# An attention block and a Fourier block on one core: down-projection in steps of 4, 1 and 1 tiles, tables, key buffer, head 0 operands and weights moved, products on unused PSUM banks around the transforms

## The chip, the cores and the metric

The kernel runs on one core of one Trainium2 chip. A core has four compute engines with instruction streams of their own (TensorE, VectorE, ScalarE, GpSimd) and SyncE (SP), which here issues nearly all transfers on one queue served by 16 DMA engines. The metric is device microseconds of one execution; less is better. In names of rows PE is TensorE, DVE VectorE, ACT ScalarE and POOL GpSimd.

## The reference

The input is 1x48x48x192, 2304 tokens of 192 channels. The first layer is a transformer block with 12 heads of 16 channels and a decomposed relative position term; the second is a Fourier block with block-diagonal complex weights. Both end in an MLP of width 768.

```python
xn = layernorm(x, ln1_g, ln1_b)
q, k, v = split(xn @ qkv_w + qkv_b)                    # 12 heads of 16
attn = einsum('bqc,bkc->bqk', q * scale, k)
attn += rel_h[:, :, :, :, None] + rel_w[:, :, :, None, :]  # q times tables Rh, Rw
x = x + (softmax(attn) @ v) @ proj_w + proj_b
x = x + gelu(layernorm(x) @ mlp_w1 + mlp_b1) @ mlp_w2 + mlp_b2
# second layer
h = layernorm(x, g1, be1)
xf = rfft2(h)                                          # 48 x 25 modes
o = softshrink(cmul(relu(cmul(xf, w1) + b1), w2) + b2, 0.01)
h = irfft2(o) + h + x
y = h + gelu(layernorm(h) @ fc1_w + fc1_b) @ fc2_w + fc2_b
```

## The kernel before

The kernel is written by hand, an instruction stream for each engine, with counted semaphores between them. Each engine works in order. Nearly every product is made in float16 pairs: a value is a rounded part (`hi`) and a rest (`lo = x - hi`), and hi and lo have products of their own.

*Stage 1, queries, keys, values.* The tokens come in NC = 6 chunks of 384. VectorE normalises (`norm_chunk`; the inverse root is GpSimd's `norm_root`), TensorE transposes, ScalarE applies gain and bias, TensorE makes keys, queries and values, ScalarE rounds keys and queries into `khl`, VectorE subtracts, and SP stores both parts to DRAM as `kq_d`; `columns_first` on GpSimd makes a copy of the queries in column order (`qw_d`). SP reads the queries back, three heads' worth on 96 partitions (`q_h`, `q_w`). In the first chunks ScalarE and VectorE also prepare the relative tables `rel` (`table_hi`, `table_parts`, `table`); their 12 loads and the 3 of `mask` are issued by ScalarE. In SBUF, `khl` and `rel` lie where the staging tiles `stage` of stage 2 lie.

*Stage 2, relative terms.* For s = 0 to 3 (6 heads by rows, 6 by columns, and again), 8 tiles each, TensorE multiplies queries with tables, ScalarE rounds to `stage_hi`, VectorE subtracts to `stage_lo`, and SP stores both to `rel_d` (2.65 MB for each s). s = 2 needs the tiles of s = 0 stored, s = 3 those of s = 1.

*Stage 3, the heads.* First the maximum of each row of scores is found: units of products of `qc` and `kc` (queries with relative terms, keys with one-hot rows), reduced by VectorE into `mx_p`; the maxima pass through DRAM (`m_d`, function `m_through_dram`) into a row of `qv`. Then, in three quarters of 18 steps for each head, scores from `ka` and `qv`, an exponential on ScalarE, and products with `v_ext`. Between the steps run the maximum units of the next quarter. SP loads the operands of the next quarter or head at counts of `s_ps`, a step each. The MLP weights are loaded before head 0's second quarter, and GpSimd scales and splits them.

*Stage 4, first MLP and width transform* (`block0`), 6 chunks: `up` makes 6 hidden tiles, ScalarE does gelu and `hi`, and the engine that runs `lo_of_hidden` the rest; `down` multiplies. In between stand the projection and normalisation of the next chunk. `down` before starts so:

```python
pe.wait_ge(sems["hi"], (c + 1) * HM - 1)   # 5 of 6 tiles
for t in (0, 2): hi_products(t, range(HM - 1))
pe.wait_ge(sems["hi"], (c + 1) * HM)
```

*Stage 5, transforms along the height and the complex products*, 5 groups of 5 modes, with a way through DRAM before (`u1_d`) and after (`u2_d`). *Stage 6, second MLP* (`block1`), like stage 4, where GpSimd subtracts 4 of the 6 hidden tiles (POOL_TILES) and VectorE 2.

## Time and profile before

| | us |
|---|---|
| median of 3 runs (1145.84 to 1151.11) | 1150.13 |
| the profiled execution | 1151.58 |
| its span | 1149.8 |
| TensorE busy | 1013.9 (88%) |
| VectorE busy | 844.1 (73%) |
| ScalarE busy | 700.7 (61%) |
| GpSimd busy | 181.0 (16%) |
| mean granted clock of TensorE | 0.937 |

The span goes from the first instruction to the last; 1.8 us of the execution lie around it. A clock of 1.00 is 2.4 GHz, 0.50 is 1.2 GHz. Stage 1 lasts to about 74 us, stage 2 to 122, the maxima before head 0 run from 130 and its scores from 159, the heads end at 833, the first MLP at 955, the transforms at 1054. A busy share is a mean over stages with different limits, so each stage has to be read alone.

### The profile page before, as it was taken

The numbers are of one execution on the slowest core, as the hardware profiler recorded it, in microseconds if no ns is written. First come the engines' busy times: TensorE is split into PE (matmuls) and PEld (weight loads), VectorE is DVE, ScalarE is ACT, GpSimd is POOL, SyncE is SP. The second block draws the span as 40 slices with busy tenths as digits, with TensorE's granted clock in tenths as the row PEclk, the third lists the DMA queues.
The fourth block names the chain that finished last, engine by engine and source line by source line (L and its number), as shares of the span: only waits on it lengthen the run. The fifth ranks groups of instructions, "written<-read, shape, count | busy, mean of one in ns | idle before, by whom it ended". The sixth has DMA issues, their size and how long they took to land.

```text
span 1149.8 us, 35628 instructions
## 1 busy us (share of the span) xinstructions
PE 1013.9 (88%) x15434; PEld 725.3 (63%) x15434; DVE 844.1 (73%) x1702; ACT 700.7 (61%) x1002; POOL 181.0 (16%) x154
## 2 busy tenths in 40 slices
PE   4867588999999999999999999999987884984997
PEld 2545135667777776777777776777476763862776
DVE  2846677999999998999999999999246562232442
ACT  3646126777777777778777777777853450322554
POOL 2540008200000000000000000000046461001443
PEclk9985569999999999999999999999999997995999
DMA  8498697656475656566574756646000012111110
GB/s 120 120 248 263 205 174 125 116 91 116 89 120 95 108 93 105 101 96 112 86 122 87 126 85 113 98 79 108 26 11 22 22 32 56 39 45 45 38 38 21
DMA packets 83234, 109.14 MB, mean 95 GB/s; under 512 B 14334, under 2 KB 75459, under 8 KB 82886
## 3 DMA queue, kind: packets, MB, share of 16 engines
q1 hardware_dynamic: 82550, 105.10, 47.3%
q10 hardware_dynamic: 528, 1.77, 1.2%
q8 instruction: 121, 1.98, 0.8%
q14 instruction: 35, 0.29, 0.1%
HBM read 85.40 MB, written 21.44 MB: 93 GB/s over the span
## 4 chain that ended last, share of the span: by engine, by line
PE 74%; DVE 8%; DMA 7%; ACT 4%; issue 2%; POOL 2%; SPq 1%; ACTq 1%; DVEq 0%
PE ps L1003 36%; PE ps L998 18%; PE ps L1157 17%; DVE mx_p L1446 3%; DVE xh L101 2%; ACT hid_f L930 2%; POOL hid L746 1%; PE ps L1011 1%; DVE stage_lo L1418 1%; DMA mask<-in_c_mask 1%; ACT hid L924 1%; DMA m_d<-mneg 1%; DMA rel_d<-stage_lo 1%; PE ps L1103 1%; POOL rstd L109 1%
## 5 line engine op out<-in xcount | busy, mean ns | idle before, releaser
L1446 DVE TENSOR_REDUCE mx_p<-ps 128x1 f32<-128x464 f32 (+1 forms) x1080 | 608.5, 629 | 43.4 <-PE ps L1003 32.5
L880 ACT ACTIVATE prob<-ps 128x768 f32<-128x768 f32 x648 | 496.0, 810 | 194.5 <-PE ps L1003 193.6
L1003 PE MATMUL ps<-kc,qc 112*32 112x464 f16 (+1 forms) x4320 | 463.0, 370 | 15.2 <-DMA qc<-rel_d 11.2
L1003 PE MATMUL ps<-qv,ka 113*32 113x384 f16 x5184 | 405.6, 328 | 13.4 <-DMA qv<-m_d 5.9
L1157 PE MATMUL ps<-prob,v_ext 128*32 128x384 f32 x2592 | 294.5, 487 | 2.0 <-issue 1.5
L1003 PEld LDWEIGHTS ps<-qv,ka 113*32 113x32 f16 x5184 | 217.6, 97 | 88.7 <-issue 30.3
L1003 PEld LDWEIGHTS ps<-kc,qc 112*32 112x32 f16 x4320 | 176.5, 95 | 112.8 <-issue 31.6
L1157 PEld LDWEIGHTS ps<-prob,v_ext 128*32 128x32 f32 x2592 | 118.4, 111 | 16.4 <-issue 3.5
L998 PE MATMUL ps<-w_dn,hid 128*96 128x192 f16 x864 | 78.2, 251 | 13.9 <-ACT hid L924 13.1
L998 PEld LDWEIGHTS ps<-w_dn,hid 128*96 128x96 f16 x864 | 74.5, 126 | 18.7 <-ACT hid L924 16.2
L719 POOL COPY v_ext<-v_all 128x288 f32<-128x288 f32 x12 | 5.1, 428 | 512.8 <-PE ps L1157 512.7
L998 PE MATMUL ps<-xnt_all,w_up 96*128 96x384 f16 x432 | 76.9, 331 | 3.0 <-ACT xnt_all L872 2.2
L746 POOL TENSOR_TENSOR hid<-hid_f,hid 128x384 f16<-128x384 f32 x60 | 59.7, 1003 | 73.1 <-ACT hid L924 72.0
L930 ACT ACTIVATE hid_f<-ps,b_up 128x384 f32<-128x384 f32 x72 | 40.6, 580 | 42.3 <-PE ps L998 42.2
L998 PEld LDWEIGHTS ps<-xnt_all,w_up 96*128 96x128 f16 x432 | 42.2, 99 | 33.9 <-issue 5.8
L109 POOL TENSOR_TENSOR rstd<-rstd 96x4 f32<-96x4 f32 x24 | 24.3, 1013 | 218.4 <-DVE rstd L96 218.0
L868 ACT ACTIVATE xnt_f<-ps,shift,gain 96x384 f32<-96x384 f32 x24 | 14.7, 662 | 64.1 <-PE ps L1011 64.1
L1011 PE MATMUL ps<-ident,xh 96*96 96x96 f32 x144 | 17.9, 276 | 33.3 <-DVE xh L101 24.8
L1424 DVE TENSOR_TENSOR xnt_all<-xnt_f,xnt_all 96x768 f16<-96x768 f32 x12 | 11.5, 955 | 45.1 <-ACT xnt_all L872 45.1
L1418 DVE TENSOR_TENSOR stage_lo<-ps,stage_hi 96x864 f16<-96x864 f32 x32 | 31.2, 1045 | 16.6 <-ACT stage_hi L856 16.6
L856 ACT ACTIVATE stage_hi<-ps 96x864 f16<-96x864 f32 x32 | 27.1, 894 | 21.2 <-DMA kq_d<-khl 8.2
L1011 PEld LDWEIGHTS ps<-ident,xh 96*96 96x96 f32 x144 | 14.4, 142 | 37.0 <-DVE xh L101 19.2
(103 smaller groups left out, 821.1 us busy)
## 6 DMA issues: line engine op xcount, KB each, us to landing
qv<-rel_d SPq DMA_DIRECT2D x216, 144.0 KB
qv<-kq_d SPq DMA_DIRECT2D x108, 216.0 KB
qc<-rel_d SPq DMA_DIRECT2D x24, 216.0 KB, 4.1
xin<-in_x SPq DMA_DIRECT2D x12, 288.0 KB, 3.8
kq_d<-khl SPq DMA_DIRECT2D x24, 144.0 KB, 2.3
q_h<-kq_d SPq DMA_DIRECT2D x9, 288.0 KB, 4.7
q_w<-qw_d SPq DMA_DIRECT2D x9, 288.0 KB, 6.9
rel_d<-stage_hi SPq DMA_DIRECT2D x4, 648.0 KB, 8.4
```

The source lines that it names most:

```text
L101: ins = nc.vector.tensor_scalar(dst[:, t, :], src[:, t, :], mv[:, t, 0:1], rstd[:, 1, t:t + 1], ALU.subtract, ALU.mult)
L109: nc.gpsimd.tensor_tensor(rstd[:, 1, :], rstd[:, 0, :], rstd[:, 2, :], ALU.pow).then_inc(sem["rstd"], 1)
L746: nc.gpsimd.tensor_tensor(hid[:, m, 1, :], hid_f[:, m, :], hid[:, m, 0, :], ALU.subtract).then_inc(sems["lo"], 1)
L856: nc.scalar.activation(out_hi[0], x, ACT.Copy).then_inc(op_hi, 1)
L880: nc.scalar.activation(prob[:, s4(p, s), :].rearrange("p (a b) -> p a b", a=2), ps[:, 3 + 2 * (s % 2):5 + 2 * (s % 2), 0:CW], ACT.Exp).the ...
L930: nc.scalar.activation(hid_f[:, m, :], ps[:, m % 2, 0:CW], ACT.Gelu, bias=b_up[i][:, m:m + 1], scale=1 / WS).then_inc(sems["act"], 1)
L998: return nc.tensor.matmul(o, l, r, start=start, stop=stop)
L1003: ins = nc.tensor.matmul(ps[c:c + 32, bank, 0:w], l[:, c:c + 32], r, start=True, stop=True, tile_position=(0, c))
L1011: ins = nc.tensor.transpose(ps[0:C2, bank + k, t * T:(t + 1) * T], src[:, t, k * C2:(k + 1) * C2], ident[0:T, 0:T])
L1157: ins = nc.tensor.matmul(ps[r:r + 32, 7, 0:CW], v_ext[:, p, (s + e) % GS, :], prob[:, s4(p, s + e), j * CW:(j + 1) * CW], start=(s % GS == ...
L1418: nc.vector.tensor_tensor(out_lo, x, out_hi, ALU.subtract).then_inc(op_lo, 1)
L1446: nc.vector.tensor_reduce(mx_p[:, q * GT + k // MP, k % MP:k % MP + 1], ps[:, slot, 0:min(MW, N - k % MP * MW)], AX, ALU.max).then_inc(uni ...
```

## The change

1. The tables come in one load each and the mask in one, all from SP; ScalarE's 15 loads are gone, and a small first activation on ScalarE stands at its start. `table_hi` and `table_parts` move from chunks 0 and 1 to 1 and 2, `table` from chunks 2 to 5 to chunks 3, 3, 4, 5.
2. `khl` has a place of its own. The waits of ScalarE and VectorE for its stores ahead of stage 2 are gone, and query stores come before key stores, with semaphores of their own.
3. `qc` and `kc` are split by head parity, with the first pair on a place that is free in stage 2. One-hot rows for head 0 are loaded ahead of the stores; its `qc` waits for s = 0 and 1 alone.
4. MLP weights are loaded within head 0, two at a time; other weights, transforms and filters one head later.
5. `block0` shares its subtractions as `block1` did, 4 on GpSimd and 2 on VectorE beside the root, and GpSimd's `skip` goes behind `bias_into`.
6. `down` waits for 4, 5 and 6 hidden tiles.
7. `stay_awake` multiplies `hid` with itself into banks that nobody reads, at six places.

```diff
+        with ExitStack() as r:
+            khl = sb("khl", [C2, 2, 4, 2, CW], F16, r)
...
+        with ExitStack() as r:
+            qc0, kc0 = (sb(n, [128, N], F16, r) for n in ("qc0", "kc0"))
...
+            def load_table(i):
+                table = (d["c_rel_h"], d["c_rel_w"])[i]
+                sp.dma_start(rel[i][:, :, :].rearrange("p x y -> p (x y)"),
+                             table[0:HD].rearrange("c x y -> c (x y)").unsqueeze(0)
+                             .to_broadcast([6, HD, S * S])).then_inc(rel_in[i], 16)
...
+                if c < 2:
+                    load_table(c)
                 sp.wait_ge(kq_lo, c * 4 + 4)
-                for i in range(4):
+                for i in (2, 3, 0, 1):
...
+                    if is_at(n, 0):
+                        load_mlp(q - 1, step + M_STEP + 3)
+                    if is_at(n, 1) and q == 1:
                         load_weights(sp)
...
+            onehot_c(0)
+            for half in range(2):
+                sp.wait_ge(op_lo, (half + 1) * OT // 2)
+                store_rel(0, slice(half * N // 2, (half + 1) * N // 2))
+            sp.wait_ge(op_lo, 2 * OT)
+            store_rel(1, slice(0, N))
+            sp.wait_ge(op_lo, 2 * OT + OT // 2)
+            store_rel(2, slice(0, N // 2))
+            for c in range(2):
+                sp.wait_ge(k_out[c], 32 * NC // 2)
+            sp.wait_ge(q_out[0], STORES[0])
+            sp.wait_ge(q_out[1], STORES[1])
+            load_c(0, 0)
+            sp.wait_ge(op_lo, 3 * OT)
+            store_rel(2, slice(N // 2, N))
+            sp.wait_ge(q_out[0], 2 * STORES[0])
             load_k(0, 0)
             load_qv(0, 0, 0)
+            onehot_k(0)
+            sp.wait_ge(op_lo, 4 * OT)
+            store_rel(3, slice(0, N))
+            onehot_k(1)
+            sp.wait_ge(q_out[1], 2 * STORES[1])
+            onehot_c(1)
             m_through_dram(0, 0, 0, before.index(("mt", 0, 0)) + 1)
...
-                lo_of_hidden(c, up0)
+                lo_of_hidden(c, up0, range(POOL_TILES))
                 if more:
                     norm_root(pool, nc, rstd, ln2, c + 1)
+                    bias_into(c + 1, 0, ln2, x1b_ok)
                 if not is_at(c, 0):
                     skip(c - 1)
-                if more:
-                    bias_into(c + 1, 0, ln2, x1b_ok)
...
+            act.wait_ge(exponent, 1)
+            nc.scalar.activation(f_wn[:, 0, 0:CT], rstd[:, 2, :], ACT.Copy)
...
-            for p in range(2):
-                act.wait_ge(kq_out[p], 64 * NC // 2)
...
+            def stay_awake(count, bank, x):
+                for _ in range(count):
+                    mm(ps[:, bank, 0:CW], x[:, 0:128], x[:, 0:CW])
...
-                pe.wait_ge(sems["hi"], (c + 1) * HM - 1)
...
+                for tiles in (range(HM - 2), range(HM - 2, HM - 1), range(HM - 1, HM)):
+                    pe.wait_ge(sems["hi"], c * HM + tiles.stop)
+                    for t in (0, 2):
+                        hi_products(t, tiles)
...
+            stay_awake(34, 4, hid[:, 0, 0, :])
             dft(NC - 1)
+            stay_awake(44, 4, hid[:, 0, 0, :])
...
+            stay_awake(14, 3, hid[:, 0, 0, :])
             inverse(G - 1)
+            stay_awake(42, 3, hid[:, 0, 0, :])
...
             inverse_w(0)
+            stay_awake(30, 3, hid[:, 0, 0, :])
             norm_transposed(0, ln4, t4_ps)
+            stay_awake(8, 3, hid[:, 0, 0, :])
```

What the instructions look like at three places follows. On SP's queue before the change, from the second half of the stores of s = 2 to the maxima of head 0 (`kc<-in_c_onehot_c` and `ka<-in_c_onehot` are the one-hot rows):

```order
L569 DMA rel_d<-stage_lo 96x3x1152
L577 DMA kc<-in_c_onehot_c 96x2304 x2
L503 DMA qc<-kq_d 16x2304
L503 DMA kc<-kq_d 16x2304
L503 DMA qc<-rel_d 48x2304 x2
L569 DMA rel_d<-stage_hi 96x3x2304
L569 DMA rel_d<-stage_lo 96x3x2304
L593 DMA ka<-in_c_onehot 16x2304 x4
...
L532 DMA qv<-rel_d 32x3x768 x6
L538 DMA m_d<-mneg 6x128
```

The same stretch of the changed kernel's queue:

```order
L522 DMA qc<-kq_d 16x2304
L522 DMA kc<-kq_d 16x2304
L522 DMA qc<-rel_d 48x2304 x2
L590 DMA rel_d<-stage_hi 96x3x1152
L590 DMA rel_d<-stage_lo 96x3x1152
...
L551 DMA qv<-rel_d 32x3x768 x6
L600 DMA ka<-in_c_onehot 16x2304 x4
L602 DMA ka<-in_c_onehot 1x2304
L590 DMA rel_d<-stage_hi 96x3x2304
L590 DMA rel_d<-stage_lo 96x3x2304
...
L594 DMA kc<-in_c_onehot_c 96x2304
L557 DMA m_d<-mneg 6x128
```

Head 0's `qc` moved ahead of half a stage of stores, `qv` ahead of the stores of s = 3, and the maxima's write stayed last. On GpSimd, one middle chunk of the first MLP before (`rstd` is the root, `r<-h,y_sb` is `skip`, `x<-x,rows` is `bias_into`):

```order
L746 TENSOR_TENSOR hid<-hid_f,hid 128x384 x6
L109 TENSOR_TENSOR rstd<-rstd 96x4
L769 TENSOR_TENSOR r<-h,y_sb 96x768
L753 TENSOR_TENSOR x<-x,rows 96x768
L109 TENSOR_TENSOR rstd<-rstd 96x4
```

The same chunk of the changed kernel on GpSimd:

```order
L779 TENSOR_TENSOR hid<-hid_f,hid 128x384 x4
L109 TENSOR_TENSOR rstd<-rstd 96x4
L786 TENSOR_TENSOR x<-x,rows 96x768
L801 TENSOR_TENSOR r<-h,y_sb 96x768
L109 TENSOR_TENSOR rstd<-rstd 96x4
```

Two subtractions left GpSimd, and `skip` now stands behind the wait of `bias_into` for VectorE's `xh`. On TensorE, around the last width transform (`h,dft_w`) and the first height transform of the changed kernel:

```order
L1023 MATMUL ps<-w_dn,hid 96x192 x72
L1023 MATMUL ps<-h,dft_w 100x384 x2
L1023 MATMUL ps<-hid 128x384 x34
L1023 MATMUL ps<-h,dft_w 100x384 x2
L1023 MATMUL ps<-hid 128x384 x44
L1023 MATMUL ps<-dft_h,f_in 96x96 x10
```

The two rows of `hid` are new; the others stood in this order before.

## Rows read from the trace of the kernel before

**Rows 1.** Windows: engines' busy us (instructions), clock, DMA share, GB/s

```profile
74.00:130.00 56.00, 27.10 (x192) 21.55 (x192) 31.49 (x33) 27.06 (x32) 3.23 (x6) 0.55 0.86 239
...
224.00:833.00 609.00, 599.79 (x11804) 429.64 (x11804) 560.22 (x1090) 473.07 (x632) 7.15 (x12) 1.00 0.59 98
...
955.00:1054.00 99.00, 63.88 (x427) 49.52 (x426) 27.45 (x59) 20.76 (x40) 5.64 (x4) 0.78 0.18 50
```

**Rows 2.** Chain that ended last: start, us, what; then ScalarE and VectorE timelines

```profile
13.44 13.01 DMA mask<-in_c_mask
...
73.87 6.19 DMA kq_d<-khl
...
82.41 8.33 DMA q_w<-qw_d
...
109.70 11.55 DMA rel_d<-stage_lo
...
123.50 6.83 DMA qc<-rel_d
...
130.46 0.60 PE ps L1003 x3
...
150.68 5.64 DMA m_d<-mneg
...
159.08 5.06 PE ps L1003 x52
...
113.28 6.87 ACT L856 ACTIVATE stage_hi<-ps 96x864 f16<-96x864 f32 x8 [7.00 <-DMA rel_d<-stage_lo]
...
114.27 7.81 DVE L1418 TENSOR_TENSOR stage_lo<-ps,stage_hi 96x864 f16<-96x864 f32 x8 [6.06 <-ACT stage_hi L856]
```

**Rows 3.** Timelines, stage 1: start, us, engine, instruction, [idle before, releaser]

```profile
16.13 0.67 ACT L812 ACTIVATE xnt<-ps,shift,gain 96x384 f32<-96x384 f32 x1
...
39.61 2.61 DVE L1390 SCALAR_TENSOR_TENSOR rel_hi<-rel_hi,mask,rel 96x2304 f16<-96x2304 f16 x1
...
44.00 0.88 DVE L1405 COPY v_all<-ps 128x192 f32<-128x192 f32 x3
...
51.93 0.88 DVE L1405 COPY v_all<-ps 128x192 f32<-128x192 f32 x3
```

**Rows 4.** DMA issues (count, KB each, us to landing); TensorE timeline, head 0

```profile
w_dn_f<-in_L_conv_fc_w SPq DMA_DIRECT2D x1, 576.0 KB, 16.8
...
181.41 0.50 PE L1003 MATMUL ps<-qv,ka 113*32 113x384 f16 x6 [4.61 <-issue]
```

**Rows 5.** Timelines, first MLP: TensorE, VectorE, GpSimd

```profile
833.10 2.12 PE L998 MATMUL ps<-xnt_all,w_up 96*128 96x384 f16 x12
...
884.90 3.17 PE L998 MATMUL ps<-w_dn,hid 128*96 128x192 f16 x36 [1.08 <-ACT hid L924]
890.49 0.86 PE L1011 MATMUL ps<-ident,xh 96*96 96x96 f32 x8 [2.41 <-DVE xh L101]
891.19 4.79 PE L998 MATMUL ps<-w_dn,hid 128*96 128x192 f16 x36
...
938.94 2.11 PE L998 MATMUL ps<-xnt_all,w_up 96*128 96x384 f16 x12
...
887.71 2.72 DVE L101 TENSOR_SCALAR xh<-x,mv,rstd 96x192 f32<-96x192 f32 x4 [2.82 <-POOL rstd L109]
...
887.65 1.80 POOL L769 TENSOR_TENSOR r<-h,y_sb 96x768 f32<-96x768 f32 x1
```

**Rows 6.** Timelines, second MLP: TensorE, VectorE

```profile
1080.15 3.17 PE L998 MATMUL ps<-w_dn,hid 128*96 128x192 f16 x36 [1.08 <-ACT hid L924]
...
1080.13 1.03 DVE L1538 TENSOR_TENSOR hid<-hid_f,hid 128x384 f16<-128x384 f32 x2 [1.94 <-ACT hid L924]
1081.12 1.25 DVE L101 TENSOR_SCALAR xh<-x,mv,rstd 96x192 f32<-96x192 f32 x4
```

**Rows 7.** TensorE timeline around the transforms

```profile
953.59 1.46 PE L998 MATMUL ps<-h,dft_w 96*100 96x384 f32 x4
961.48 2.85 PE L998 MATMUL ps<-h,dft_w 96*100 96x384 f32 x4 [6.43 <-DVE h L1512]
...
1031.47 3.24 PE L998 MATMUL ps<-f_o,dft_h 96*96 96x384 f32 x6 [3.19 <-DVE f_o L1532]
...
1050.75 1.52 PE L1011 MATMUL ps<-ident,xh 96*96 96x96 f32 x8 [5.41 <-DVE xh L101]
1054.46 4.02 PE L998 MATMUL ps<-xnt_all,w_up 96*128 96x384 f16 x12 [2.19 <-ACT xnt_all L872]
```

**Rows 8.** Windows, first group of the height transform

```profile
972.00:984.00 12.00, 10.63 (x56) 8.85 (x56) 0.43 (x2) 2.74 (x6) 0.00 (x0) 0.64 0.14 40
```

133 lines of the change are left out of this document (63 added, 70 removed).

## Prediction

> **What bounds the kernel now.** I read the page first, then the busy time by stage, then the chain that ended last, then the timelines of single engines. The span is 1149.8 us and the profiled execution took 1151.6, that is 1.8 outside the span; the median of the other runs is 1150.13, 1.4 under the profiled one, so a sum made against 1151.6 may be high by about 1. The stage windows [rows 1] say where nothing can be won: from 224 to 833 TensorE is busy 599.79 of 609 us at full clock, and the change leaves those heads alone. The other 541 us are 0 to 224 and 833 to the end; of them 74 to 130 has TensorE busy for 27.10 of 56 us at a mean clock of 0.55 with the DMA engines at 0.86, and the transforms, 955 to 1054, have it busy for 63.88 of 99 us at 0.78. A measurement of this kernel tells a difference from about 0.5%, some 6 us.
>
> **Before head 0.** The chain [rows 2] waits 13.01 us for the mask, 6.19 for a store of keys and queries, 8.33 for a load of q_w, 11.55 for a store of rel_d, 6.83 for qc and 5.64 for the maxima written to DRAM.
>
> *Start.* ScalarE issues 15 loads, then loads its function table, so its first scaling starts at 16.13 [rows 3]. In the new order it has only to wait for the transposes, which VectorE and TensorE finish near 10.3: first products at 14.2 and not 19.9. The wait for tables and mask (26.45 us) no longer holds chunk 0. After that VectorE sets the pace: from one copy of v_all to the next it is 7.93 us (44.00 to 51.93), and a pass over a table adds 2.61 [rows 3]; both passes now lie in chunks 1 and 2, one of them hidden before under the late start. From first products at 14.2, five slow microseconds and v at 24 the copies of v_all end at 25.0, 35.9, 46.7, 54.9, 61.0, 68.3; the third ended at 52.8 before (51.93 + 0.88). So the stage gains 46.7 against 52.8, **-6.0**. Two passes of `table` in chunk 3 cost ScalarE 2.2 more; it has 3 us to spare there, because VectorE is still at its normalisation. The bounds are -9 (all of the first chunk's gain kept) and 0.
>
> *The tables' new shape.* One load now brings a whole table with a source of 6 blocks of 16 rows. The second is issued near 28 and needed near 41; the four MLP weight loads, 2.3 MB, had all landed 16.8 us after the last was issued [rows 4], about 140 GB/s, by which 0.88 MB take 6.5 us, so it hides. The Trainium skill (DMA: Bandwidth & Descriptors, "Why a DMA increments its semaphore by 16 and not by 1") says that a transfer uses the largest number of engines up to 16 that divides the slowest dimension of both sides, which would be 6 here. No run here shows it yet. As a mechanism of this kernel it is a rival below.
>
> *Queries first.* The last store of queries passes ahead of the keys, and its wait covers only itself. The q_h load was issued at 80.12, right after the 6.19 us row; it can't be issued before the last qw_d store, about 3.8 earlier. With the DMA engines at 0.86 [rows 1] an earlier issue is partly an earlier place in a full queue, so I take **-1.5**, between 0 and -3.8. That ScalarE no longer waits for the stores (five tiles early) hides behind q_w, which the next tiles need anyway.
>
> *Operands of head 0.* qc was loaded after all of stage 2 was stored (109.70 + 11.55 = 121.26) and behind both one-hot blocks, so the maxima started at 130.46 [rows 2]. Now it waits only for stages 0 and 1, landed at 113.2 [rows 2], and the maxima start when VectorE ends stage 3: 8 tiles of 0.98 from 114.27, 122.1 before, and 7.5 less, 114.6, now. They and the 5 behind them need the old 20.2 us (130.46 to 150.68), so the first row maxima are ready at 135. But the queue is now: qc and kc, second half of stage 2, ka and qv, stage 3, one-hots, and the write of the maxima stands behind the wait for stage 3's landing. Stage 2 lands at 115; ka and qv (1.7 MB, before at about 10 us) until 126; stage 3 (2.65 MB, 8.5 us of busy engines) until 137.5; one-hot, write and read-back 6.6 us: scores start at 144.1 and not 159.1. That is -15.0 in all, of which -6.0 and -1.5 are told, **-7.5** is this one. Bounds: -12 if the maxima at 135 decide, 0 if the queue keeps its old distance.
>
> **Head 0.** Four MLP weight loads (2.3 MB) stood ahead of qv; the last landed after 16.8 us, and TensorE stood 4.61 us in "issue" at 176.80 with the DMA engines full [rows 4]. They now go two at a time at the end of the quarters' steps. I take the 4.61, and 1.4 for the clock that fell in that pause (half speed until 185): **-6.0**; bounds 0 (the stall moves to the quarter that gets them) and -7. The 12, 6 and 16 small loads move one head later, into quarters that have about 40% of DMA time free: nothing; without that cover 5 us of SP's issue. GpSimd's weight preparation, 28 us, comes later by a quarter and is needed 600 us on: nothing.
>
> **First MLP.** Chunks 0 to 4 take 105.84 us, from the first up products at 833.10 to those of the last chunk at 938.94 [rows 5]. The third shows why. TensorE ends the up products at 883.8, waits for hid until 884.90 (1.08), works 3.17, waits 2.41 for xh, transposes, then takes 4.79 for 36 products, as many as before took 3.17 at full clock. xh is late because GpSimd does six hid subtractions before the root, and VectorE's four operations then take 2.72 beside GpSimd's `r<-h,y_sb`; in the second MLP they take 1.25 [rows 6]. Afterwards: down products begin at once (-1.08); GpSimd's fourth subtraction ends at 884.8 and the root at 885.9; VectorE's two take 1.03 [rows 6] and end at 886.0; xh at 887.3 and not 890.4, against TensorE's free moment at 887.0; the clock stays up (-1.6). The chunk's TensorE work is 9.25 up with the projection, 6.64 down with transposes, 1.46 of transform, with 0.4 waits 17.7; VectorE's own round is 17.9: addition to root 4.05, xh 1.25, a wait for TensorE and ScalarE 3.1, input 0.95, sum to h 8.5. I take 17.9 for chunks 1 to 4 and 16.9 for chunk 0, which has no transform and no h behind it: 88.5, and 105.84 - 88.5 = 17.3; the last gains its 1.08 and little more, 1.2. **-18.5**; bounds -10 (a chunk of 19.9, when VectorE's round grows by 2) and -20.
> The row of 2.72 against 1.25 is what the Trainium skill (GPSIMD Engine Reference, Specifications) calls contention with VectorE instructions that take two SBUF inputs or a 2-port mode. It speaks against putting subtractions of two SBUF tiles on VectorE; by it the two might take GpSimd's 1.8 and not 1.03, 0.8 a chunk more, while rows 6, with GpSimd busy beside them, show 1.03.
>
> **Transforms.** The shape of 4 passes of 96x384 took 1.46 at 953.59 and 2.85 at 961.48 [rows 7]: behind 6.43 idle the clock is at 1.2 and not 2.4 GHz. I walk the chain with full clock. A filler product has the up products' shape, 0.17 each (2.11 for 12 at 938.94 [rows 5]). 34 of them from 955.9 end at 961.7, 0.4 after h is ready; the transform then costs 1.46: -1.0. 44 take 7.5, and the spectrum's way through DRAM, from 964.3 to 972, 7.65: just covered. From 972 to 984 [rows 8] 10.63 us of products ran at half clock for most of it; all at full they lose 3.8. 14 fillers (2.4) fit the 3.19 wait at 1031.47, the inverse takes 1.86 and not 3.24: -1.4. 42 take 7.1 and lie under a like way through DRAM; the next product costs 1.46 for 2.85: -1.4. 30 take 5.1, under the next normalisation; the transposes behind it take 0.86 [rows 5] and not 1.52: -0.7. 8 take 1.4 of the 2.19 before 1054.46, and the first up products 2.11 for 4.02: -1.9, the next one -0.4. Sum **-10.7**. Bounds: 0, if the gaps that are left let the clock fall all the same, and -12.
> The Trainium skill (TensorE: Matmul & The Clock Gate, Part 1) says that the clock falls after idle and returns after sustained work; the trace agrees, 2.85 against 1.46.
>
> **Second MLP.** The 1.08 wait goes six times [rows 6], but xh, paced by ScalarE, ends at 1082.37 where the down products had ended at 1083.2, so five chunks gain 0.7 and the last 1.0: **-4.5**; bounds -2 and -6.5.
>
> **Sum.** 6.0 + 1.5 + 7.5 + 6.0 + 18.5 + 10.7 + 4.5 = 54.7; 1151.6 - 54.7 = 1096.9, so **1097 us**.
>
> **Rivals.** (a) The DMA queue eats its part: stage 3's store and the one-hots ahead of the maxima keep the old distance, and the stall of head 0 moves on. Neither 7.5 nor 6.0 comes: 1110. For: 0.86 in 74 to 130 [rows 1]; against: the qc load and both one-hots moved with the stores waiting for nothing else. 17%. (b) The first MLP becomes VectorE's: h's two operations at 1.55 beside GpSimd, and skip after bias holds y_sb, chunk 19.6: 4 x 1.7 = 7 less, 1104. 12%. (c) The fillers don't hold the clock, or run past the data: 1107. For: after 2.41 idle the clock fell at 890; against: TensorE waits of 1.08 in the second MLP [rows 6] are followed by full-clock products. 10%. (d) The tables come over few engines: at 6/16 of 140 GB/s the second takes 17 us, lands near 45.5, 4.5 late against 41: 1101. 8%. (e) Other side: the key buffer, qc and kc lie elsewhere in SBUF; if that made each of the 36 quarters (18.8 us) of the heads longer by more than 1.5 us, all 54.7 is gone and the kernel slower. Nothing in rows of products or loads points to placement. 2%. (f) No effect worth measuring: 1%. Forecast as worked: 50%.
>
> **Numbers.** The forecast's own spread is about 9 either way, from the bounds of the DMA part and of the MLP taken together; rivals (a) to (d) lie 4 to 13 above. I take 1086 to 1111. Faster 0.97, same 0.01, slower 0.02.
>
> **What would show it.** Right: first scaling near 10.3, scores from 144, no pause of 4 us near 165, chunks of 18 us with xh of 1.25, clock above 0.95 from the first MLP on through the transforms, second MLP chunks of 14.3. Wrong: a wait for qv<-m_d beyond 147, a ScalarE wait for rel in chunk 2, a filler that ends after the data it precedes, or a head longer than 56.5 us.

## The result and the profile after

The changed kernel takes 1114.59 us (median of 4 runs, 1113.01 to 1115.95) against 1150.2 (4 runs): ratio 0.9697, 95% interval 0.9669 to 0.9725. It is faster, by 35.6 us and not by the 54.7 of the forecast, and 3.6 us above the range. The profiled execution took 1113.01, its span is 1111.2, against 1149.8: 38.6 us less. The windows of the changed kernel, by stage; columns as in [rows 1].

```profile
70.00:117.00 47.00, 26.77 (x192) 21.24 (x192) 31.30 (x33) 26.67 (x32) 3.14 (x6) 0.54 0.92 266
...
146.30:210.00 63.70, 59.14 (x1064) 40.50 (x1068) 52.99 (x100) 42.67 (x56) 14.88 (x5) 0.93 0.71 133
...
818.80:931.60 112.80, 102.49 (x856) 80.87 (x852) 71.30 (x171) 52.63 (x99) 54.99 (x44) 0.98 0.09 23
935.00:1026.00 91.00, 84.39 (x602) 62.06 (x601) 26.07 (x50) 21.82 (x42) 4.72 (x4) 1.00 0.19 52
```

The transforms run at clock 1.00 where [rows 1] had 0.78. The stretch before head 0 is as starved as it was. The timelines of the changed kernel up to head 2 (ScalarE, VectorE, SP, TensorE) answer to [rows 2 to 4]:

```profile
10.14 0.67 ACT L838 ACTIVATE xnt<-ps,shift,gain 96x384 f32<-96x384 f32 x1 [2.38 <-PE ps L1041]
...
38.62 2.12 ACT L849 ACTIVATE rel_hi<-rel 96x2304 f16<-96x2304 f32 x1 [3.81 <-DMA rel<-in_c_rel_w]
...
69.28 0.89 DVE L1443 COPY v_all<-ps 128x192 f32<-128x192 f32 x3 [0.89 <-PE ps L1023]
...
140.59 0.33 SPq L557 DMA_DIRECT2D m_d<-mneg  x1
143.68 0.78 SPq L559 DMA_DIRECT2D qv<-m_d  x1
...
164.60 0.42 SPq L634 DMA_DIRECT2D w_up_f<-in_L_conv_mlp_w  x1
165.86 0.41 SPq L636 DMA_DIRECT2D w_dn_f<-in_L_conv_mlp_w  x1
...
186.75 0.42 SPq L634 DMA_DIRECT2D w_up_f<-in_L_conv_fc_w  x1
...
146.33 0.83 PE L1028 MATMUL ps<-qv,ka 113*32 113x384 f16 x8 [4.40 <-DMA qv<-m_d]
...
177.93 0.37 PE L1028 MATMUL ps<-kc,qc 112*32 112x448 f16 x3 [2.54 <-issue]
...
199.44 0.52 PE L1189 MATMUL ps<-prob,v_ext 128*32 128x384 f32 x2 [1.99 <-issue]
...
248.47 0.51 PE L1028 MATMUL ps<-qv,ka 113*32 113x384 f16 x8 [2.27 <-DMA qv<-m_d]
```

ScalarE's first gain comes at 10.14, as forecast, but it waits 3.81 us for the second table. The pause of 4.61 [rows 4] has become two pauses in issue (idle time of TensorE in which it waited for nothing that the profile shows), each ending 13 us behind the issue of a pair of MLP weight loads, and a wait for the maxima's way through DRAM.

By quarters, from the first scores of one to those of the next, head 0 took 27.64, 18.20 and 19.52 us before and takes 20.03, 20.91 and 22.33 now; head 1 took 55.95 and takes 58.23. The first quarter gained 7.6, more than was hoped, and the next five gave all of it back.

A chunk of the first MLP, changed kernel, timelines of TensorE, VectorE and GpSimd (before: [rows 5]):

```profile
856.26 2.11 PE L1023 MATMUL ps<-xnt_all,w_up 96*128 96x384 f16 x12
...
868.63 1.19 PE L1023 MATMUL ps<-w_dn,hid 128*96 128x192 f16 x12 [0.72 <-DVE hid L1540]
870.77 0.87 PE L1041 MATMUL ps<-ident,xh 96*96 96x96 f32 x8 [0.95 <-DVE xh L101]
...
875.74 2.11 PE L1023 MATMUL ps<-xnt_all,w_up 96*128 96x384 f16 x12
...
855.64 0.94 DVE L1532 SCALAR_TENSOR_TENSOR y_sb<-ps,x 96x768 f32<-96x768 f32 x1
...
859.63 2.65 DVE L101 TENSOR_SCALAR xh<-y_sb,mv,rstd 96x192 f32<-96x192 f32 x4 [1.13 <-POOL rstd L109]
...
864.78 0.95 DVE L1470 TENSOR_TENSOR x<-ps,xin 96x768 f32<-96x768 f32 x1
...
867.56 1.02 DVE L1540 TENSOR_TENSOR hid<-hid_f,hid 128x384 f16<-128x384 f32 x2
869.47 1.24 DVE L101 TENSOR_SCALAR xh<-x,mv,rstd 96x192 f32<-96x192 f32 x4 [0.90 <-POOL rstd L109]
873.81 1.37 DVE L1463 TENSOR_TENSOR xnt_all<-xnt_f,xnt_all 96x768 f16<-96x768 f32 x1 [3.10 <-ACT xnt_all L897]
...
859.69 0.91 POOL L779 TENSOR_TENSOR hid<-hid_f,hid 128x384 f16<-128x384 f32 x1
861.26 1.80 POOL L779 TENSOR_TENSOR hid<-hid_f,hid 128x384 f16<-128x384 f32 x2 [0.66 <-ACT hid L949]
...
867.72 1.71 POOL L109 TENSOR_TENSOR rstd<-rstd 96x4 f32<-96x4 f32 x1 [1.12 <-DVE rstd L96]
```

From one addition to x to the next VectorE takes 19.48 us (845.30 to 864.78), without a wait for TensorE; TensorE waits for it twice. Chunks 0 to 4, by the starts of their up products, take 17.37, 20.12, 19.48, 19.48 and 21.13 us; in the last of them the second half of the down products runs at the low clock (4.54 us for 36, against 3.13). Two shapes of four operations, alike in size, take 2.65 and 1.24: the first has GpSimd at work beside it.

The transforms and the second MLP, TensorE's timeline of the changed kernel (before: [rows 7], [rows 6]):

```profile
932.46 5.70 PE L1023 MATMUL ps<-hid 128*128 128x384 f16 x34 [0.90 <-ACT u_sb L966]
938.00 1.46 PE L1023 MATMUL ps<-h,dft_w 96*100 96x384 f32 x4
939.29 7.32 PE L1023 MATMUL ps<-hid 128*128 128x384 f16 x44
947.29 1.91 PE L1023 MATMUL ps<-dft_h,f_in 96*96 96x96 f32 x20 [0.68 <-DMA f_in<-u_d]
...
1065.56 2.12 PE L1023 MATMUL ps<-xnt_all,w_up 96*128 96x384 f16 x12
...
1079.89 2.12 PE L1023 MATMUL ps<-xnt_all,w_up 96*128 96x384 f16 x12
```

The product that took 2.85 takes 1.46. Five of the six groups of fillers end 0.5 to 0.9 us before the data that they precede; the first ends 0.5 us behind it (h is ready at 937.52, its product starts at 938.00). A chunk of the second MLP takes 14.33.

### The profile page after: what moved, and what is told of

The parts are those of the page before. It is cut to its first block, busy times and chain, and to the rows that moved or that the text cites. A ratio compares the mean times of both kernels' runs of the same rounds, so it can differ in the third digit from the quotient of the medians.

```text
span 1111.2 us, 35967 instructions
## 1 busy us (share of the span) xinstructions
PE 1033.5 (93%) x15606; PEld 731.5 (66%) x15606; DVE 847.2 (76%) x1714; ACT 700.6 (63%) x1003; POOL 170.7 (15%) x142
## 4 chain that ended last, share of the span: by engine, by line
PE 71%; DVE 12%; DMA 7%; ACT 5%; issue 3%; POOL 2%; SPq 0%; DVEq 0%; ACTq 0%; POOLq 0%
PE ps L1028 35%; PE ps L1189 17%; PE ps L1023 15%; DVE mx_p L1485 4%; DVE xh L101 2%; POOL rstd L109 1%; DMA m_d<-mneg 1%; DVE stage_lo L1454 1%; PE ps L1041 1%; ACT hid_f L955 1%; DVE stats L88 1%; DMA rel_d<-stage_lo 1%; DMA rel<-in_c_rel_w 1%; PE ps L1135 1%; DMA qv<-m_d 1%
## 5 line engine op out<-in xcount | busy, mean ns | idle before, releaser
L1028 PEld LDWEIGHTS ps<-qv,ka 113*32 113x32 f16 x5184 | 213.9, 97 | 86.7 <-issue 28.6
L1028 PEld LDWEIGHTS ps<-kc,qc 112*32 112x32 f16 x4320 | 173.2, 95 | 108.0 <-DVE mx_p L1485 30.0
L109 POOL TENSOR_TENSOR rstd<-rstd 96x4 f32<-96x4 f32 x24 | 27.5, 1145 | 211.5 <-DVE rstd L96 211.2
L779 POOL TENSOR_TENSOR hid<-hid_f,hid 128x384 f16<-128x384 f32 x48 | 45.5, 953 | 69.0 <-ACT hid L949 68.0
L949 ACT ACTIVATE hid<-hid_f 128x384 f16<-128x384 f32 x72 | 35.9, 516 | 0.0
```

The costliest lines, as they stand in the source:

```text
L109: nc.gpsimd.tensor_tensor(rstd[:, 1, :], rstd[:, 0, :], rstd[:, 2, :], ALU.pow).then_inc(sem["rstd"], 1)
L779: nc.gpsimd.tensor_tensor(hid[:, m, 1, :], hid_f[:, m, :], hid[:, m, 0, :], ALU.subtract).then_inc(sems["lo"], 1)
L949: nc.scalar.activation(hid[:, m, 0, :], hid_f[:, m, :], ACT.Copy).then_inc(sems["hi"], 1)
L1028: ins = nc.tensor.matmul(ps[c:c + 32, bank, 0:w], l[:, c:c + 32], r, start=True, stop=True, tile_position=(0, c))
```

## The experiments

All edits are to the changed kernel. "Chunks 0 to 4" is the time from the first up products of the first MLP to those of its last chunk (before 105.84, forecast 88.5, changed kernel 818.77 to 916.35 = 97.58). "Heads" is the time from the first scores to the first up products (before 674.02, changed kernel 672.44). Each batch of runs was measured beside the kernel before, whose medians were 1149.7 to 1152.9.

Two spreads bound what one profile can show. Nine profiled kernels have the changed kernel's code in the heads, itself included: their heads took 670.3 to 677.0, and their two pauses in issue in head 0 1.7 to 5.3 and 1.6 to 3.4. Nine have its code in the first MLP: their chunks 0 to 4 took 95.9 to 97.6.

### What paces the first MLP

**h one chunk later.**

```diff
 projected(c + 1, 6, lambda: lo_of_hidden(c, up0, tiles))
+if c > 0: scaled(c - 1)      # h's multiplication and addition, from the end of the block
 lo_of_input(c + 1, 0)
```

> Changed kernel, but in the first MLP VectorE computes h of chunk c-1 (its multiplication and addition, 2.5 us with the transition) only after the projected sum of chunk c+1 is normalised, where VectorE waited 3.10 us for ScalarE (869.47 + 1.24 to 873.81). Theory A (VectorE's own round paces the chunk: 19.5 us, of which a wait of 3.1 and no wait for TensorE): the round loses about 2, chunks 1 to 4 take 17.5 to 18.0, the first MLP (818.77 to 931.56, 112.79 us) loses 6 to 8, the kernel takes 1107 to 1109. Rival B (the chunk is paced by TensorE with the transposes and the clock, VectorE only follows): the projected sum would then wait for TensorE as before, chunks stay at 19.5, 1114. Rival C (GpSimd paces it, its skip now stands behind a later h and holds the sum of the down products): chunks of 19 or more, and a wait of the sum for r3.

Measured: 1111.59 us (1110.95 to 1112.66); chunks of 18.96, chunks 0 to 4 in 92.32. Between A and C: the round got shorter, but the sum of the down products now waited for GpSimd's `skip`, which reads the same y:

```profile
877.23 0.95 DVE L1532 SCALAR_TENSOR_TENSOR y_sb<-ps,x 96x768 f32<-96x768 f32 x1 [1.79 <-POOL r L801]
```

**The same with two y buffers**, in the sum, the normalisation and `skip`.

```diff
+y_two = (y_sb, sb("y_sb1", [T, CT, C]))
-mlp_sum(c, up0, x1b_ok, lambda: wait_used(dve, r3_ok, c))
+mlp_sum(c, up0, x1b_ok, lambda: wait_used(dve, r3_ok, c - 1), y_two[c % 2])
```

> h of chunk c-1 after the normalisation of chunk c+1, as in the run that moved it alone, and a second buffer for y in the first MLP. With h moved alone chunks took 18.96 us (876.24 to 895.20), and VectorE's sum of the down products waited 1.79 us for GpSimd's skip addition, which reads the same y buffer (877.23 0.95, idle 1.79 for r). Theory A (that wait is what is left of the VectorE round over 17.2): chunks 1 to 4 take 17.3 to 17.9 and the first MLP is 5 to 7 us shorter than with h moved alone; the kernel takes 1104 to 1107. Rival B (TensorE or the contention of VectorE and GpSimd, 3.09 us for four operations that take 1.25 alone, has the next word): chunks of 18.3 or more, 1109 or more.

Measured: 1104.42 (1102.79 to 1107.79), ratio to before 0.9603 (0.9571 to 0.9636). Chunks of 18.07 (872.67 to 890.75), chunks 0 to 4 in 89.67. The time is A's, the chunk lies between A's and B's. VectorE now waits for TensorE:

```profile
880.05 0.95 DVE L1471 TENSOR_TENSOR x<-ps,xin 96x768 f32<-96x768 f32 x1 [2.35 <-PE ps L1024]
```

So the chunk that TensorE paces is 18.07, and what lay above it was VectorE's.

**One wait on GpSimd.**

```diff
 def block0(c, more):               # GpSimd
+    if c > 0: pool.wait_ge(ln3["out"], c)
     lo_of_hidden(c, up0, range(POOL_TILES))
```

> Changed kernel in which GpSimd waits, in the first MLP, for the normalised y of the chunk before (VectorE's four xh operations) before it starts the subtractions of hid. In the changed kernel these four take 2.65 to 3.03 us while GpSimd subtracts beside them (859.63 and 840.38), and 1.24 where it does nothing (869.47). Nothing else is moved; the fourth subtraction waits for ScalarE anyway. Theory A (two engines at work on SBUF slow each other, and VectorE paces the chunk): the four take 1.25, the chunk of 19.5 loses 1.1 to 1.4, the first MLP 5 to 7 us, the kernel takes 1108 to 1110. Rival B (xh of y is slow by its operands or by its buffer, whatever GpSimd does): 2.65 to 3.03 stay, 1114, or 1115 by the later subtractions.

Measured: 1110.2 (1107.79 to 1116.14); chunks of 18.08, chunks 0 to 4 in 90.54. That is 7.0 less than in the changed kernel's profile and 5.4 to 7.0 less than in the nine with the same first MLP; the median fell by 4.4, and the heads of this profile took 676.3, within their spread. VectorE, then GpSimd in this kernel:

```profile
861.89 1.24 DVE L101 TENSOR_SCALAR xh<-y_sb,mv,rstd 96x192 f32<-96x192 f32 x4 [1.13 <-POOL rstd L109]
...
865.89 0.95 DVE L1472 TENSOR_TENSOR x<-ps,xin 96x768 f32<-96x768 f32 x1 [0.18 <-PE ps L1025]
...
863.21 4.14 POOL L779 TENSOR_TENSOR hid<-hid_f,hid 128x384 f16<-128x384 f32 x3 [1.36 <-DVE xh L101]
```

Theory A holds: an added wait took the 2.65 to 1.24, and VectorE is back to waiting for TensorE. GpSimd's subtractions now overlap h's two operations and take 4.14 for three, where three took 2.69 in the changed kernel (at 840.32), but GpSimd has the time. The Trainium skill (SBUF — State Buffer, "SBUF: two separate sides") says that VectorE in a 2-port mode, or with two SBUF inputs, and GpSimd lock a shared port pair for a whole instruction, the other one blocking; the numbers fit that, no run here shows the lock itself.

**The share of the subtractions undone.**

```diff
-lo_of_hidden(c, up0, range(POOL_TILES))      # GpSimd; VectorE's part is taken out
+lo_of_hidden(c, up0)
 norm_root(pool, nc, rstd, ln2, c + 1)
-bias_into(c + 1, 0, ln2, x1b_ok)
 skip(c - 1)
+bias_into(c + 1, 0, ln2, x1b_ok)
```

> Changed kernel with one part undone in the first MLP: all six subtractions of hid are GpSimd's again, and its skip addition stands ahead of the bias. The down products keep their order of 4, 1, 1 tiles. It prices that part. Theory A (the share between the engines is what gained the 9.2 us of the first MLP, and the slow clock in each chunk came from the wait for xh): the first MLP takes 119 to 122 us, 6 to 9 longer, the kernel 1121 to 1124, and a wait of about 2.4 for xh with 36 down products of 4.5 us or more is back in the chunks. Rival B (the 4, 1, 1 order gained it, the share nothing): no more than 2 us longer.

Measured: 1132.69 (1131.55 to 1135.27), 18 us more than the changed kernel and over twice what A had. Chunks of 23.74, longer than any of before's (18.7, 22.7, 22.6, 20.9 and 20.9):

```profile
877.94 1.51 PE L1042 MATMUL ps<-ident,xh 96*96 96x96 f32 x8 [2.53 <-DVE xh L101]
879.25 5.37 PE L1024 MATMUL ps<-w_dn,hid 128*96 128x192 f16 x36
```

The wait for xh is as in [rows 5], but two shorter pauses (0.20, 0.59) now stand ahead of it, and transposes and products both run at the low clock (1.51 and 5.37 against 0.86 and 4.79 there, and 3.13 where the clock is full). The share, with the order of bias and `skip` that was undone beside it, is worth 4.3 us a chunk once `down` starts early. And the early start alone, without the share, costs 1 to 3 us in each chunk after the first: xh comes as late as it did, TensorE stands idle in three places ahead of it, and the clock falls in all of these chunks, where before it fell only in the two of 22.7 and 22.6.

**Down's waits as before, 5 and 1.**

```diff
-for tiles in (range(HM - 2), range(HM - 2, HM - 1), range(HM - 1, HM)):
+pe.wait_ge(sems["hi"], (c + 1) * HM - 1)
+for tiles in (range(HM - 1), range(HM - 1, HM)):
```

> Changed kernel with one part undone: the down products of both MLPs wait for five tiles of hid and then for the sixth, as before, and not for 4, 1 and 1. It prices that part, and says what the early start does to the clock. Theory A (as in the prediction: it saves a wait of 1.08 in every chunk): where VectorE paces the first MLP it changes nothing there, the second MLP takes 81.2 + 4 = 85, the kernel 1118 to 1119. Rival B (in the first MLP the early start only makes the pauses before the low products longer, 0.72 to 1.37 us, and costs clock): the first MLP is 1 to 3 us shorter with the old order and the kernel takes 1115 to 1117.

Measured: 1120.46 (1118.31 to 1121.92). The first MLP's chunks stay at 19.48 (chunks 0 to 4: 96.19, within the spread), those of the second take 15.10 (1041.79 to 1056.89) and not 14.33. A in mechanism, the median 1.5 above its range: the early start gains nothing where VectorE paces, 0.76 a chunk where it doesn't.

### The fillers

```diff
-stay_awake(34, 4, hid[:, 0, 0, :])      # and the five others
```

> Changed kernel without all 172 filler products on unused banks. Theory A (they gain by the clock alone, worked out as 10.7 and seen as 98.4 us for the transforms against 110.1): 931.6 to 1030 becomes 108 to 110 us, the products behind each pause take 2.8, 3.2 and 4.0 us again, the granted clock of 935 to 1026 is near 0.8, the kernel takes 1124 to 1126. Rival B (the gain came from the first MLP handing over at full clock, so part of it stays without fillers): 4 to 6 us longer only, 1119 to 1121.

Measured: 1126.63 (1121.38 to 1129.12), 12.0 more. The windows row and two TensorE rows without them:

```profile
935.00:1026.00 91.00, 66.63 (x418) 52.48 (x418) 21.78 (x36) 18.28 (x36) 1.80 (x1) 0.75 0.19 50
```

```profile
1031.65 1.51 PE L1041 MATMUL ps<-ident,xh 96*96 96x96 f32 x8 [5.40 <-DVE xh L101]
1035.36 4.02 PE L1023 MATMUL ps<-xnt_all,w_up 96*128 96x384 f16 x12 [2.19 <-ACT xnt_all L897]
```

These are before's durations [rows 7]: A's mechanism, it is the fillers that hold the clock. The size went beyond A's: in this profile, the slowest of the four runs, the transforms took 113.9 (932.13 to 1046.05), 15.5 more than with fillers and more than the 110.07 of before, which had the full clock in more of them (0.78 in [rows 1] against 0.75).

### The tables

```diff
-sp.dma_start(rel[i], table[0:HD].unsqueeze(0).to_broadcast([6, HD, S * S]))
+for b in range(6):
+    sp.dma_start(rel[i][b * HD:(b + 1) * HD, :, :], table[0:HD]).then_inc(rel_in[i], 16)
```

> Changed kernel with each relative-position table loaded by six transfers of 16 rows in place of one transfer with a repeated source. Theory A (the one transfer keeps few engines busy, so that the second table lands 11.2 us after its issue at 27.35): the second table lands within 7 us, ScalarE's pass over it starts at 35.7 to 36.5 and not at 38.6, and the last copies of v_all end 1.5 to 2.5 us earlier than 70.17; the kernel gains 1 to 2.5 us. Rival B (0.88 MB take 11 us beside the other loads and stores whatever the shape, or five more issues of 0.45 us on the queue take it back): the pass stays at 38 or later and the kernel at 1114.

Measured: 1114.32 (1108.18 to 1120.19). ScalarE and VectorE:

```profile
35.73 2.12 ACT L848 ACTIVATE rel_hi<-rel 96x2304 f16<-96x2304 f32 x1 [0.58 <-DMA rel<-in_c_rel_w]
...
67.23 0.89 DVE L1442 COPY v_all<-ps 128x192 f32<-128x192 f32 x3 [0.89 <-PE ps L1022]
```

The mechanism is A's: the pass starts 2.9 earlier, the last copies of v_all 2.05 (69.28 to 67.23). How many DMA engines the one load kept busy can be read where it was the only one under way, in a window from 31 to 33 us, first the changed kernel, then this one:

```profile
31.00:33.00 2.00, 1.96 (x15) 1.59 (x14) 2.00 (x4) 0.54 (x1) 0.00 (x0) 1.00 0.37 129
...
31.00:33.00 2.00, 1.99 (x16) 1.77 (x15) 2.00 (x3) 0.20 (x1) 0.00 (x0) 1.00 0.98 180
```

A share of 0.37 is that of 6 engines out of 16; from 17 to 20 us, beside the first table, it is 0.38 against 0.91. The engine count that the prediction cited from the Trainium skill (DMA: Bandwidth & Descriptors, "Why a DMA increments its semaphore by 16 and not by 1") agrees with it. The whole kernel's runs spread over 12 us, which hides 2.

### Head 0 and 1

**The maxima's write ahead of the one-hots and the last wait for stores.**

```diff
+m_through_dram(0, 0, 0, before.index(("mt", 0, 0)) + 1)
 onehot_k(1)
 sp.wait_ge(q_out[1], 2 * STORES[1])
 onehot_c(1)
-m_through_dram(0, 0, 0, before.index(("mt", 0, 0)) + 1)
```

> Changed kernel with the write of head 0's first maxima through DRAM issued ahead of the one-hot rows of head 1 and ahead of the wait for stage 3's stores. In the changed kernel the maxima are ready at 137.4, the write is issued at 140.59, scores start at 146.33. Theory A (the write waits in SP's order only): it is issued near 137.5 and scores start 2.5 to 3.2 us earlier, the kernel takes 1111 to 1112. Rival B (the write and its read-back stand behind the bytes of stage 3 in the DMA queues anyway): issued near 137.5 but scores start no more than 1 us earlier, 1114.

Measured: 1116.09 (1111.34 to 1121.89). Scores start at 143.09, 3.2 earlier (A), but the one-hot and qc loads that it passed now stand in head 0, whose pauses in issue were 1.68, 4.36 and 3.43, and in the profiled run, the slowest of the four, the heads took 682.5. The median shows no gain. That the passed loads took it back is argued; the four runs spread over 10.5 us.

**One MLP weight load a quarter.**

```diff
-if is_at(n, 0): load_mlp(q - 1, step + M_STEP + 3)                          # two loads
+if is_at(n, 0) or is_at(n, 1):
+    load_mlp(int(not is_at(n, 0)), q - 1, step + M_STEP + 3)                # one load
```

> Changed kernel with the four MLP weight loads of 576 KB each in a quarter of its own (two quarters of head 0, two of head 1) in place of two and two in head 0; GpSimd prepares the weights after the copies of v for heads 2 and 3. In the changed kernel TensorE stands 2.54 us in issue at 177.93 and 1.99 at 199.44, each 11 to 13 us after a pair of loads, with the DMA engines at 1.0 and above and one instruction packet in the stretch, and then 2.27 us for qv<-m_d at 248.47. Theory A (full DMA engines delay the fetch of the next instructions): with half the bytes a quarter the engines don't fill as long, both issue pauses fall under 1 us, heads 0 and 1 are 3 to 5 us shorter, the kernel takes 1110 to 1111. Rival B (the pauses are there at certain places of the program whatever is loaded): pauses stay at about 178 and 199, 1114. Rival C (the qv loads alone fill the engines): pauses in other quarters.

Measured: 1116.08 (1112.23 to 1116.99). Pauses of 0.83 and 1.77 in issue, waits of 1.73 and 2.34 for qv<-m_d; heads 668.4 in the profile, the fastest of the four runs. A in part in the trace, nothing in the median; inconclusive.

**The MLP loads in heads 4 and 5.**

```diff
+if n in (4, 5): load_mlp(n - 4, q - 1, step + M_STEP + 3)
```

> Changed kernel with the four MLP weight loads in heads 4 and 5, one a quarter, and GpSimd's preparation of them in head 7. In heads 0 and 1 nothing of them is left. Theory A (it is the loads on top of head 0's own transfers that make the pauses of 2.54 and 1.99 us in issue, and the preparation on GpSimd changes nothing): no pause over 0.7 us is left between 150 and 240, none appears in heads 4 and 5, scores to the end of the heads (672.44 in the changed kernel, 668.4 with one load a quarter) become 666 to 668, the kernel takes 1109 to 1111. Rival B (pauses of instruction fetch belong to heads 0 and 1 anyway, by the transfers for qv, qc and kc): 670 or more, the kernel at 1113 to 1116.

Measured: 1116.29 (1114.69 to 1117.47), heads 675.2. Quarters 2 to 4 fell to 18.12, 18.17 and 18.15, a wait of 2.08 for the maxima at the start of head 2 stayed, and the pauses came back behind three of the four loads, issued at 404.85, 445.28 and 464.51:

```profile
417.89 0.37 PE L1033 MATMUL ps<-kc,qc 112*32 112x448 f16 x4 [2.95 <-issue]
458.36 0.37 PE L1033 MATMUL ps<-kc,qc 112*32 112x464 f16 x1 [1.34 <-issue]
480.90 0.59 PE L1194 MATMUL ps<-prob,v_ext 128*32 128x384 f32 x3 [2.86 <-issue]
```

Neither A nor B, though the time is B's: the pause goes where the load goes.

**The small loads late too**, behind the write of the maxima.

```diff
+if n in (2, 3, 6, 7, 8):
+    for dst, src in small[k * 34 // 10:(k + 1) * 34 // 10]: load(sp, dst, src)   # k counts the quarters
```

> As the run before it, and the 34 small loads (weights' rows, transforms, filters) in heads 2, 3, 6, 7 and 8, three or four a quarter, in place of 12, 6, 8 and 8 in the quarters of heads 1 and 2. In the changed kernel TensorE waits 2.27 us for qv<-m_d at 248.47. Theory A (the 12 and 6 loads in one quarter push the qv loads and the write of the maxima late on SP's queue, 5 to 6 us of issue): this wait goes, another 2 us, heads 664 to 666, the kernel 1107 to 1109. Rival B (the wait stems from GpSimd's or the DMA queue's other work): no difference to the run with the MLP loads alone moved.

Measured: 1117.28 (1116.43 to 1121.23). The wait for qv<-m_d at head 2 is gone, but a pause of 2.20 at 304.79 came, and those of heads 4 and 5 stayed. A in mechanism, B in time.

**All of this together**: tables in six transfers, late loads, h later with two buffers, and GpSimd's wait.

> Everything that helped or should help together: six transfers for each table, the loads of both kinds in later heads, h one chunk later with a second y buffer, and GpSimd's subtractions after xh. If the parts add up from the changed kernel's 1114.6: tables 2, loads 6, first MLP 10 by the run with two y buffers. Theory A: 1096 to 1099. Rival B (the heads' pauses don't go, only move): 1101 to 1104.

Measured: 1105.01 (1102.08 to 1109.72): nearest to B, a microsecond above it, and no better than the two y buffers alone. The pause at 415.84 is 3.50 here, that at 458.44 2.40.

**One extra 576 KB load in each of eight quarters** (heads 3, 6, 7, 8).

```diff
+sp.wait_ge(s_ps, step + M_STEP + 3)
+sp.dma_start(extra[:, :, :], d["L0_conv_mlp_w2"].rearrange("(k p) n -> p k n", p=128))
```

> Changed kernel with one more load of an MLP weight (576 KB, into a tile that nobody reads) in each of the eight quarters of heads 3, 6, 7 and 8, at step 16; the output is the same. Theory A (each such load costs TensorE a pause in issue of 1 to 3 us, wherever it is): 8 to 20 us more, 1123 to 1134, with quarters of 19.5 to 21 in these heads. Rival B (a quarter of a later head has room for 576 KB and hides it): no more than 3 us.

Measured: 1122.74 (1112.45 to 1128.27), 8.2 more, 1.0 us a load. In the profiled run, the slowest, the heads took 687.8, 15.3 more, but 5.5 of that lies in heads 0 and 1, which have no extra load. Of the eight quarters right behind the loads five were longer by 1.3 to 2.3 and three by nothing, 8.8 in all. A at its lower edge, except that not every load costs.

**The same MLP loads at another place of the quarter.**

```diff
 load_qv(n, q, (p + q) % 2, step)
+if is_at(n, 0) or is_at(n, 1):
+    load_mlp(int(not is_at(n, 0)), q - 1, step + 9)   # one of the four, behind qv
 m_through_dram(n, p, q, units_to(n, "mt", q))
```

> Changed kernel with one MLP weight load a quarter in heads 0 and 1, issued at step 10 of the quarter behind its qv loads, and not at step 16 and 18 right ahead of the next quarter's qv loads; GpSimd's preparation as in the run with one load a quarter at step 16. Theory A (pauses in issue come from the collision of a 576 KB load with the nine qv loads behind it): no pause over 0.7 us in heads 0 and 1, the four quarters take 18.2 and not 20.6, 21.0, 22.2, the kernel 1108 to 1110. Rival B (the price is that of the bytes, wherever they lie in the quarter): pauses of 1 to 3 us again, some 10 us behind each load, or a wait for qv<-m_d, 1113 to 1116.

Measured: 1110.84 (1108.68 to 1111.38), heads 667.9. No pause in issue in heads 0 and 1, where the same four loads at the end of their quarters left 0.83 and 1.77; the quarters after the first take 18.1, 19.2 and 18.2. A, but a wait for the maxima is left at the start of head 2:

```profile
234.60 0.27 SPq L557 DMA_DIRECT2D m_d<-mneg  x1
241.27 0.71 SPq L559 DMA_DIRECT2D qv<-m_d  x1
...
243.89 0.83 PE L1033 MATMUL ps<-qv,ka 113*32 113x384 f16 x8 [3.93 <-DMA qv<-m_d]
```

**The small edits together**: tables in six and GpSimd's wait; then with the loads in mid quarter; then with the 34 small loads in mid quarter of heads 3 to 7.

```diff
     load_mlp(int(not is_at(n, 0)), q - 1, step + 9)
+if n in (3, 4, 5, 6, 7):
+    for dst, src in small[k * 34 // 10:(k + 1) * 34 // 10]: load(sp, dst, src)
 m_through_dram(n, p, q, units_to(n, "mt", q))
```

> Changed kernel with only the two small edits that helped: six transfers for each table, and GpSimd waiting for the normalised y before it subtracts. Theory A (they add up: tables 2.0, first MLP 5.6, both seen in the traces): 1106 to 1108. Rival B (the two microseconds of the tables are lost again in head 0, whose start is set by other transfers): 1109 to 1110.

> Six transfers for each table, GpSimd's wait in the first MLP, and the MLP weight loads in the middle of their quarters. Theory A: 1101 to 1104. Rival B (the place of the loads gives nothing): 1106 to 1109.

> The best kernel so far (six transfers for each table, GpSimd's wait in the first MLP, MLP weight loads at step 10 of four quarters), and the 34 small loads three or four a quarter at the same place of heads 3 to 7. Theory A (the small loads in the quarters of head 1 hold the read-back of the maxima: written at 234.60, read-back issued at 241.27, TensorE waits 3.44 to 3.93 us at the start of head 2): this wait goes, no other comes, the kernel takes 1097 to 1099 beside 1101.6. Rival B (it stems from the MLP load that is issued 2.5 us ahead of the write): the wait stays and the kernel at 1101 or more. Rival C (small loads cost wherever they stand, as when they stood at step 13 and later of heads 2, 3 and 6 to 8): pauses in heads 3 to 7, 1101 to 1104.

Measured: 1107.69 (1104.66 to 1109.96), 1101.61 (1098.04 to 1104.84) and 1097.78 (1092.05 to 1101.9), each A. The last has a ratio to before of 0.9518 (0.9488 to 0.9549), heads of 665.2 and, at the start of head 2, no wait over 0.7 us. One pause of 1.93 in issue at 302.90 is in it, and one of 0.8 to 2.4 near 524 to 549 in every kernel here, that of before included, with a bulk load ahead of it in only one; so a pause in issue does not need such a load, and what makes these stays open. In the profile of this last kernel the fillers did not hold the clock everywhere: it was 0.97 from 935 to 1026, and from the last transform of the first MLP to the second's first up products 95.8 us went by, against 92.5 in the kernel without the spread loads.

## Why the prediction was wrong, term by term

The span lost 38.6 of 54.7 us; the 16.1 that are missing lie so:

| term | forecast | measured | from |
|---|---|---|---|
| start, stage 1 | -6.0 | -4.1 | last v_all copies end 74.27, now 70.17 |
| queries first | -1.5 | -0.45 | q_w products start 90.78, now 86.23 |
| operands of head 0 | -7.5 | -8.2 | scores start 159.08, now 146.33 |
| head 0 | -6.0 | -1.6 | heads 674.02, now 672.44 |
| first MLP | -18.5 | -9.2 | 121.95, now 112.79 |
| transforms | -10.7 | -10.8 | 110.07, now 98.40, less 0.9 that belongs to the next row |
| second MLP | -4.5 | -4.3 | 84.68, now 81.24, plus the 0.9 |

**First MLP, the step that failed: "VectorE's own round is 17.9".** It measured 19.48, and the excess lies in three places, each beside GpSimd: from the sum of the down products to the end of h 9.14 and not 8.5 (xh 2.65, 1.84 in the kernel before), addition to root 4.70 and not 4.05 (the root takes 1.71 beside VectorE's subtractions, 1.01 alone), input 1.37 and not 0.95. Together 1.7, which is chunks 2 and 3; chunk 0 missed by 0.5, chunk 1 by 2.2 and chunk 4, with the clock down once, by 3.2, in all 9.1 on chunks 0 to 4. The clock's 1.6 that I read in the third chunk was also to be had in two of the five chunks only, since three of them already ran those products in 3.13. I had priced the subtractions by [rows 6] rightly (1.02), and looked only there for contention; it fell on the operations around them. Rival (b), "chunk 19.6", named the engine that paces and the size, and had 12%; of its two reasons neither showed in the changed kernel: h's operations took 1.55 and 0.95 there as before, and `skip` held y_sb only once h came a chunk later. That its number fits is in part luck. One wait on GpSimd gives 5.4 to 7.0 of the missing 9 back in the stage, and 4.4 in the median. The mechanism that I gave for the gain itself held: undoing the share brings the wait for xh and the low clock back.

**Head 0: "they now go two at a time" at a gain of 6.** The first quarter gained 7.6, the second and third lost 5.5: that was the bound that I named, "the stall moves to the quarter that gets them". The table's 1.6 for all the heads is within their spread of 6.7, so the quarters say more than it does. Right ahead of the nine qv loads a 576 KB load was followed by a pause or a longer quarter in three of four cases (heads 4 and 5) and in five of eight (extra loads), of 1.3 to 3 us; behind the nine, in four of four, by no pause in issue. That the pause is a late fetch of instructions is argued, not shown: the profile names no releaser, and five packets of 16 KB of the instruction queue lie between 160 and 200 us, but six in the kernel without the pauses. The Trainium skill (Runtime: NRT & Kernel Launch, "Instruction fetch mechanics") says that a sequencer fetches its program in blocks of that size over a DMA queue of its own, and that crossing from block to block is mostly hidden; if these pauses are fetches, they were not hidden.

"The small loads: nothing" failed as well: head 1, which has most of them now, took 57.1 to 60.5 in the nine kernels with this code, 55.95 before and 54.5 where they stand in later heads. With them moved to mid quarter of later heads the wait at head 2 goes and the median falls from 1101.61 to 1097.78, the ratio to before from 0.9576 (0.9548 to 0.9605) to 0.9518 (0.9488 to 0.9549); the intervals just touch.

**Start.** The first gain at 10.14 was right. The step that failed is "so it hides": the second table landed 11.24 us after its issue, not 6.5, and ScalarE was ready for it 7.5 after the issue, at 34.8 and not "near 41". The third copies of v_all still ended at 46.05 (forecast 46.7); the loss showed behind them, where ScalarE, late by the wait, ran its two passes of `table` until 48.7: 55.24, 63.03 and 70.17 against 54.9, 61.0 and 68.3. Chunk 4 took 7.8 and not 6.1 with either form of the tables, with VectorE waiting 4.6 us for ScalarE (3.2 before), so "it has 3 us to spare there" was too high as well. Rival (d) was right in kind, few engines, with a landing of 11.24 and not 17. Six transfers give back 2.05, all of the 1.9 missing (45.27, 53.26, 60.99, 68.12).

**Queries first** was priced in the middle of its range; nearly all of it failed to come: q_h's load was issued at 75.69, 7.3 us after the issue of the last stores of keys and queries, before it was 7.6. The chain that ended last now runs beside it, over GpSimd's column copy, its store (71.34, landed after 5.42) and q_w's load (78.00, 8.19), which the change does not shorten.

**Operands of head 0, transforms, second MLP** came within 0.7, 0.1 and 0.2 us by the mechanisms described; the runs without fillers and with the old waits confirm two of them. The 0.1 is luck in part: the parts of that sum as printed make 10.6, and taking the fillers out cost 12.0 in the median and 15.5 in the transforms of a profile.

**The range.** I counted rivals (a) to (d) as exclusive, each 4 to 13 us above the forecast, and let the range end near the highest. They are not: what (b) speaks of came with 9.3, (d) with 1.9 and the stall of (a) with 4.4, all at once, 15.6 together, which makes 1112.6 of 1097, while (a)'s other part, the start of head 0, did not come. All four signs that the prediction gave for being wrong were there: the wait for qv<-m_d at 248.47, ScalarE's 3.81 for the table, a filler ending 0.5 behind its data (which the forecast itself had at 0.4), and heads 0 and 1 of 63.3 and 58.2 us.
